# Two packed attentions of a four-layer kernel: their pieces laid anew over the 16 steps of a batch

## The reference

```python
# second layer: attention over moments (instance norm of x comes in at the end)
q = Wq x + bq;  k = Wk kv + bk;  v = Wv kv + bv          # [128 channels, 256]
attn = softmax((q * scale)^T k)                          # per head, 8 channels
mean = attn v;  ex2 = attn (v * v);  std = sqrt(relu(ex2 - mean * mean))
out = (instance_norm(x) * std + mean) * mask

# fourth layer
q = layer_norm((zt + pos)^T);  kv = layer_norm((za + pos)^T)     # per position, over 128 channels
ctx = softmax((q Wq) (kv Wk)^T / sqrt(8)) (kv Wv)
r = ctx Wo + q;  out = (r + gelu(layer_norm(r) W1 + b1) W2 + b2)^T
```

## Time and profile before

| | us | |
|---|---|---|
| median of the runs | 2591.17 | 2588.92 to 2597.12 |
| the profiled execution | 2597.26 | its span 2595.5 |
| TensorE busy | 2261.8 | 87% |
| VectorE busy | 1783.5 | 69% |
| ScalarE busy | 1481.9 | 57% |
| GpSimd busy | 718.5 | 28% |
| exponentials L1405, each | 0.600 | 512 of them |
| maxima L1725, each | 0.684 | 512 of them |

### The profile page before, as it was taken

The page is one execution under the profiler, slowest core; times in us unless marked ns, Lnnn a source line. Parts: engine busy times, 40 slices in busy tenths (PEclk is TensorE's granted clock), DMA queues, the critical chain, the costliest instruction groups (busy, mean ns, idle before and its releaser), DMA issues. The chain is left out here.

```text
span 2595.5 us, 53248 instructions
## 1 busy us (share of the span) xinstructions
PE 2261.8 (87%) x17289; PEld 1802.1 (69%) x17289; DVE 1783.5 (69%) x4693; ACT 1481.9 (57%) x4021; POOL 718.5 (28%) x1041
## 2 busy tenths in 40 slices
PE   4999999995999999979788885899998787888896
PEld 3898989984989899969655553566665784555553
DVE  5666666667666666666577775888886654777746
ACT  2554545553555555557366765677777553666656
POOL 2111111111111111020245442666665104333200
PEclk7999999997999999989799997999999895999978
DMA  4100011000000100010000001000000000000000
GB/s 118 22 21 22 21 22 54 22 21 21 8 23 13 22 21 21 1 33 0 7 10 8 10 5 66 7 0 5 16 15 10 4 5 7 9 8 8 3 3 32
DMA packets 72941, 47.12 MB, mean 18 GB/s; under 512 B 29232, under 2 KB 71601, under 8 KB 72753
## 3 DMA queue, kind: packets, MB, share of 16 engines
q1 hardware_dynamic: 72752, 44.62, 6.5%
HBM read 41.45 MB, written 2.10 MB: 17 GB/s over the span
## 5 line engine op out<-in xcount | busy, mean ns | idle before, releaser
L1725 DVE TENSOR_REDUCE maxima<-bank 128x2 f32<-128x512 f32 x512 | 343.6, 684 | 176.3 <-PE bank L934 174.3
L1405 ACT ACTIVATE probs_t<-bank 128x512 f32<-128x512 f32 x512 | 292.0, 600 | 73.0 <-PE bank L925 68.3
L1281 ACT ACTIVATE wide_probs_t<-bank 128x256 f32<-128x256 f32 x256 | 98.5, 385 | 310.5 <-PE bank L814 308.3
L2047 POOL TENSOR_TENSOR wide_columns<-wide_pair_columns,zero 128x8 f32<-128x8 f32 x16 | 4.4, 278 | 861.4 <-DVE x L1622 816.5
L925 PE MATMUL bank<-q_packed,k_packed 32*128 32x256 f32 x1024 | 209.3, 351 | 31.3 <-ACT probs_t L1405 31.1
L1286 ACT ACTIVATE wide_probs<-bank,wide_neg_max 128x129 f32<-128x129 f32 x512 | 184.1, 365 | 84.7 <-DVE wide_neg_max L1592 80.4
L934 PE MATMUL bank<-k_packed,q_packed 32*128 32x256 f32 x1024 | 209.5, 352 | 8.3 <-DVE k_packed L1738 5.0
L1293 ACT ACTIVATE wide_heads_high<-bank,wide_columns 128x128 fp32r<-128x128 f32 x512 | 160.3, 365 | 96.6 <-PE bank L826 95.3
L925 PEld LDWEIGHTS bank<-q_packed,k_packed 32*128 32x128 f32 x1024 | 127.2, 200 | 120.7 <-ACT probs_t L1405 62.5
L1597 DVE RECIPROCAL wide_inverse<-wide_sums 128x2 f32<-128x2 f32 x256 | 42.5, 166 | 224.6 <-ACT wide_probs L1286 224.6
L1611 DVE SCALAR_TENSOR_TENSOR wide_heads_low<-bank,wide_columns,wide_heads_high 128x128 fp32r<-128x128 f32 x512 | 155.1, 344 | 40.9 <-ACT wide_heads_high L1293 35.5
(11 more groups left out here) (296 smaller groups left out, 6900.5 us busy)
## 6 DMA issues: line engine op xcount, KB each, us to landing
cn<-in_ctx SPq DMA_DIRECT2D x48, 128.0 KB, 2.0
wide_pair_weights<-in_L_xattn_wq SPq DMA_DIRECT2D x16, 256.0 KB, 2.9
wide_pair_weights<-in_L_xattn_wk SPq DMA_DIRECT2D x16, 256.0 KB, 3.3
wide_pair_weights<-in_L_xattn_wv SPq DMA_DIRECT2D x16, 256.0 KB, 3.8
wide_pair_weights<-in_L_xattn_wo SPq DMA_DIRECT2D x16, 256.0 KB, 3.6
q_packed<-max_rows SPq DMA_DIRECT2D x256, 4.0 KB
wide_ctx_rows<-in_ctx SPq DMA_DIRECT2D x4, 512.0 KB, 5.3
x<-in_x SPq DMA_DIRECT2D x4, 512.0 KB, 6.3
```

What stands on the lines that cost most here:

```text
L1405: act.activation(probs_t[j % 8][:, :], shifted_bank[j % 2][:, :], ACT.Exp, bias=0.0).then_inc(s.exp_ready, 1)
L1725: dve.tensor_reduce(maxima[pack // 2][:, b, pack % 2, :], head_scores[packed_scores(1 - u, j)][:, :].rearrange("p (a k) -> p a k", a=UNITS ...
```

## The change

- Each sum of 16 products is cut into two halves of eight, at steps `j % 4 == 2` and `3`; the semaphore is raised after the second. The waits of the sum go to the first half, so that the wait for the copy of the maxima stands at steps 10 and 2.
- Each other piece gets a step of its own as far as there are enough. Second layer: result 0 (now of batch `n-2`), placing q second half 1, k second half 2, projections 4 and 5, turnings 8 and 9, values 12, placing k first half 13, q first half 14. Fourth layer: rows turned 0, placings second half k 1, q 2, projections 4 and 5, turnings 7 and 8, values 9, placings first half k 10, q 11, heads 12, turned back 13, output product 15.
- Fourth layer: adding positions, turning, measuring and norming of rows happen one window earlier (batch `n+5` added, `n+4` turned, measured and normed by roots in window `n`), while turning back stays at batch `n+3`.
- `sums_copy` gets a fifth place, so that the first sum of a batch may be copied before the sums of the batch before are turned.
- GpSimd's order in the second layer is changed: the moments' mask work goes to batch `n-2`, the key work is cut in two around the heads, and the values' work comes last. The key sums on VectorE move from step 12 to 3.

```diff
-SCHEDULE1 = Schedule(place_k=0, project_k=2, turn=(6, 7), values=9, place_q_first=11, place_k_first=14, result=12)
-SCHEDULE3 = Schedule(place_k=1, project_k=3, turn=(6, 7), values=9, place_q_first=11, place_k_first=10, result=15)
+SCHEDULE1 = Schedule(second_q=1, second_k=2, project_q=4, project_k=5, turn=(8, 9), values=12, first_q=14, first_k=13, result=0)
+SCHEDULE3 = Schedule(second_q=2, second_k=1, project_q=4, project_k=5, turn=(7, 8), values=9, first_q=11, first_k=10, result=15)
+PLACED_ROWS, TURNED_BACK, HEADS = 0, 13, 12
+SUMS = (2, 3)
...
+def sums_place(g, u):
+    return PACKS * u if g == 0 else g
...
# TensorE
+                    if third and fourth and j == PLACED_ROWS:
+                        pe.wait_ge(s.placed, 2 * (i + 5))
+                        if following:
+                            pe.wait_ge(s.q_ready, 2 * (n + 1) + 1)
...
+                    if late and not third and j == when.result:
+                        pe.wait_ge(s.heads_ready, UNITS * (n - 1))
...
-                    if j % PACK == LAST_SUMS and (j > LAST_SUMS and core or j == LAST_SUMS and carry):
+                    if j % PACK in SUMS and (j > LAST_SUMS and core or j <= LAST_SUMS and carry):
...
-                        pe.wait_ge(s.exp_ready, HN * n + j - 3)
-                        if j == LAST_SUMS:
-                            pe.wait_ge(s.max_copied, 2 * n + (2 if core else 0))
-                        if j == TURN_MAXIMA[0] + 2 and following:
-                            pe.wait_ge(s.max_copied, 2 * (n + 1) + 1)
-                        if j == HN - 1 and third and carry:
-                            pe.wait_ge(s.heads_copied, i)
-                        for c in range(UNITS):
-                            for m in range(PACK):
+                        c = SUMS.index(j % PACK)
+                        if c == 0:
+                            pe.wait_ge(s.exp_ready, HN * n + PACK * (j // PACK))
+                            if j < LAST_SUMS:
+                                pe.wait_ge(s.max_copied, 2 * n + (2 if core else 0))
+                            if j == TURN_MAXIMA[0] + 1 and following:
+                                pe.wait_ge(s.max_copied, 2 * (n + 1) + 1)
+                            if j > HEADS and third and carry:
+                                pe.wait_ge(s.heads_copied, i)
+                        for m in range(PACK):
+                            last = pe.matmul(sum_bank[quad[m], :], v[:, c, PACK * g + m, :],
+                                             probs_t[(PACK * g + m) % 8][:, c * D:(c + 1) * D], start=c == 0, stop=c == UNITS - 1)
+                        if c:
+                            last.then_inc(s.sums, 1)
+                    if following and j == when.second_q:
+                        pe.wait_ge(s.q_ready, 2 * (n + 1) + 1)
+                        if third and fourth:
+                            pe.wait_ge(s.turned_copied, i + 5)
+                        put("q", 1, upper)
+                    if following and j == when.second_k:
+                        pe.wait_ge(s.k_ready, 2 * (n + 1) + 1)
+                        if late:
+                            pe.wait_ge(s.x_added, n - 1)
...
+                    if ahead and j == when.project_q:
+                        pe.wait_ge(s.in_ready, n + 3)
+                        if following:
+                            pe.wait_ge(s.q_ready, 2 * (n + 1) + 2)
+                        elif third and fourth:
+                            pe.wait_ge(s.turned_copied, i + 5)
...
# ScalarE
-                        if g == 0 and carry:
+                        if g == 1 and carry:
                             act.wait_ge(s.sums_turned, UNITS * n)
...
+                    if third and fourth and j == PLACED_ROWS + 1:
+                        act.wait_ge(s.turned, i + 5)
+                        after(act, s.rows_normed, i + 4)
+                        act.activation(turned_packed[:, :, :].rearrange("p k c -> p (k c)"), upper[:, :], ACT.Copy).then_inc(s.turned_copied, 1)
...
# GpSimd, fourth layer
+                if fifth:
+                    pool.wait_ge(s.loaded[1 - u], pair_turn(1, at(5), 1 - u))
+                    after(pool, s.turned, i + 5)
...
+                if fourth:
-                    pool.wait_ge(s.aggregated, 4 * (i + 4))
+                    pool.wait_ge(s.aggregated, 4 * (i + 5))
...
-                    after(pool, s.turned_back, i + 3)
+                    after(pool, s.turned_back, i + 4)
```

More of the change, by code:

```diff
@@ L954, in window @@
[L954 to L960, removed]
+                        else:
+                            after(pe, s.turned_copied, i + 4)
@@ new lines, in window @@
+                        for m in range(4):
+                            last = pe.transpose(upper[:, m * P:(m + 1) * P], placed_packed[:, m // 2, m % 2 * P:(m % 2 + 1) * P], ident[:, :])
+                        last.then_inc(s.turned, 1)
+                    if late and not third and j == when.result:
+                        pe.wait_ge(s.heads_ready, UNITS * (n - 1))
+                        if following:
+                            pe.wait_ge(s.k_ready, 2 * (n + 1) + 1)
+                        for m in range(2):
+                            for unit in range(UNITS):
+                                last = pe.transpose(lower[:, (2 * m + unit) * P:(2 * m + unit + 1) * P],
+                                                    heads_out[unit][:, m * P:(m + 1) * P], ident[:, :])
+                        last.then_inc(s.result, 1)
@@ L987, in window @@
+                    if ahead and j == when.project_k:
+                        pe.wait_ge(s.in_ready, n + 3)
+                        if following:
+                            pe.wait_ge(s.k_ready, 2 * (n + 1) + 2)
+                        pe.matmul(lower[:, 0:D], w_k, keys_in[u], start=True, stop=True).then_inc(s.k_projected, 1)
                     for unit in range(UNITS):
@@ L1017, in window @@
                         put("q", 0, upper)
[L1018 to L1025, removed]
+                    if ahead and j == when.first_k:
                         pe.wait_ge(s.k_low, n + 3)
                         if carry:
-                            pe.wait_ge(*((s.heads_taken, heads_taken(1, n)) if third else (s.x_added, n)))
+                            pe.wait_ge(s.heads_taken, heads_taken(third, n))
                         put("k", 0, lower)
[L1030 to L1040, removed]
-                        if ahead:
-                            pe.wait_ge(s.q_ready, 2 * (n + 2) + 1)
-                        elif following:
-                            pe.wait_ge(s.v_taken, n + 2)
-                        for k in range(4):
-                            last = pe.transpose(upper[:, k * P:(k + 1) * P], placed_packed[:, k // 2, k % 2 * P:(k % 2 + 1) * P], ident[:, :])
-                        last.then_inc(s.turned, 1)
-                    if third and carry and j == 13:
+                    if third and carry and j == HEADS:
                         pe.wait_ge(s.heads_taken, heads_taken(1, n))
@@ L1054, in window @@
                         last.then_inc(s.heads_turned, 1)
+                    if third and coming and j == TURNED_BACK:
+                        pe.wait_ge(s.rows_normed, i + 4)
+                        if ahead:
+                            pe.wait_ge(s.k_ready, 2 * (n + 2) + 1)
+                        else:
+                            after(pe, s.in_ready, n + 3)
+                        for m in range(4):
+                            last = pe.transpose(lower[:, m * P:(m + 1) * P], norm_packed[:, m // 2, m % 2 * P:(m % 2 + 1) * P], ident[:, :])
+                        last.then_inc(s.turned_back, 1)
                     if third and carry and j == when.result:
@@ L1352, in window @@
                 i = n - B * third
-                core, following, carry, ahead, coming, fourth = (at(o) is not None for o in (0, 1, -1, 2, 3, 4))
+                core, following, carry, ahead, coming, fourth, late = (at(o) is not None for o in (0, 1, -1, 2, 3, 4, -2))
                 for j in range(HN):
```

173 lines of the change are left out of this document (79 added, 94 removed).

## The result

The changed kernel takes 2856.93 us in the median of 4 runs (2818.72 to 2858.20), the kernel before 2592.06 in the median of 4. The ratio is 1.098, 95% interval 1.090 to 1.106: slower by a tenth, far outside the range. The profiled execution is the 2818.72 one; its span is 2817.0 us, 221.5 more than before. It is the quickest of the four: the other three took 2856 to 2858 us at a mean granted clock of 0.817 to 0.821, against 0.836 in the profiled one, so the profile shows the smallest loss of the four.

A forecast was written before the change was run, and what follows sets the result against it. TensorE was taken as fullest but stopping for other engines. First attention -11, second -8, clock -4, beginning +3, ends +0.5 total -20 us: 2577 profiled, 2571 on the median's footing; range 2552 to 2595.

The forecast's parts named there:

- Clock: Falls of TensorE's clock to the lower level, about 1.2 us each; three of four in the second attention go: -4 us.
- the other terms: First attention -11 us, second -8, beginning of the second +3, ends of both attentions +0.5.
- the small term: Second attention: three of its four falls of the clock, about 1.2 us each, taken away, -4 us.
- TensorE's work per batch: TensorE's own work in the new order: 17.9 us per batch in the first attention, 19.3 in the second.
- the wait at step 10: TensorE's first half sum waits for VectorE's copy of the maxima, 0.45 us late in both attentions.
- What remains of the stops: TensorE's stops in the new order: exponentials gone, waits left at step 10 and before the second attention's values, small ones.
- The wait for the norms: Second attention, step 13: the 2.3 us stop of the turning back for GpSimd's norms goes.
- the norms' buffers: Second attention, from step 13: late next, needing 4.5 us against TensorE's 4.6; cost 0.
- the three that I counted: First attention before the change, per batch: 0.9 us for exponentials, 0.7 before values, 0.2 before sums.
- The beginning of the second attention: Before its batch 0, a GpSimd chain is added, less overlap and a 1.5 us wait: +3 us, between -2 and +9.
- Side-by-side steps and the 0.1 us behind each half: First attention: lost overlaps 1.3 us and 0.1 x 4 for divided sums; 1.7 us more on TensorE.
- C: Rival: steps 2 and 10 each wait one maximum of 0.6 us longer, 1.2 per batch; +14, 2605 us; chance 0.14.

The follow-up runs named there:

- Kick0: Changed kernel plus 40 extra unused products in step 0 of batch 0 of each attention: 2574.52 us, ratio 0.989 to the kernel before.
- before_halves: Kernel before with nothing changed but the sums divided in two halves, their waits at the first half: 2728.75 us, ratio 1.050.
- whole_sums: Changed kernel with undivided sums at steps 3, 7, 11, 15, all else as changed: 2533.20 us, ratio 0.975 to the kernel before.

## Why the prediction was wrong, by its own steps

- **The step that failed is "Clock".** I counted the clock as a few falls that stops bring, priced them at 1.2 us each and took three away: -4 us. The true term was a loss of 240 to 280 us: the profiled spans differ by 221.5 us and the medians by 265, and to each come the 16 us that the other terms had promised. Two things should have warned me. The stretch before the second attention stands at 0.51, so each order must first win the higher level; I asked only how often it is lost. And I took the stops of TensorE for the cause of the lower level, though no row showed more than that they went together: the changed order stood at 0.50 with one stop of 0.7 us in 400 us, and the second attention with divided sums in the old order held 1.00 for 220 us with three stops in each batch. Kick0 shows that the clock is the loss; before_halves and whole_sums, the division put in and taken out by itself, show that the divided sums are its main cause (in the old order they cost the level in the first attention only).
- **Within its own bounds the small term was right.** Where the level was held, the four falls of the second attention were gone: in kick0 it stood at 1.00 from 2183 to 2485 us.
- **The rule that I weighed.** The Trainium skill, page "TensorE: Matmul & The Clock Gate", section "HAM oscillation — how this bites in real kernels", says that pauses between groups of products put the clock back each time. The 174 us at 1.00 with almost no stop agree with it; the 220 us at 1.00 with stops of 1.1 us in every batch do not bear it out for pauses of that length. It made me look for the loss in the pauses, and removing them did not keep the level.
- **TensorE's work per batch** was right in its sum, in the second attention by luck. First: 18.5 forecast, 18.7 with the burst, of which the wait at step 10 is 0.6 (0.45 forecast). Second: 20.3 forecast, 20.33 measured. There 1.0 us of the forecast were waits (0.3, 0.45, 0.15 and 0.1), and from start to start kick0 shows about 0.5: 0.3 at step 10, 0.2 before the values, 0.1 before the key placing. TensorE's own work is thus near 19.8 us and not 19.3, about half of the difference in the eight halves of the sums, 0.57 each and not 0.54. The two errors cancel.
- **What remains of the stops** was right in place. The wait for the maxima moved to step 10, 0.5 us in eleven of eleven batches of the first attention; in the second its record is 0.2 us and not 0.45. The wait for the norms is gone, the norms' buffers came in time. In the first attention of the kernel before there were two more stops than the three that I counted, for `std_t` (0.3 us in nine batches) and `k_packed` (0.2 us in seven).
- **The beginning of the second attention**, +3 forecast: from the first placed rows to batch 0 it took 53.7 us before and 53.4 after, so nothing.
- **What I gave away without weighing it**: that the division itself is a loss. Side-by-side steps and the 0.1 us behind each half stood in the sum as 1.7 us, and I set them against the stops as one parcel with the rest of the change. Taken apart, the division alone cost 1.0 and 1.1 us per batch at full clock, and the spreading of the pieces with whole sums gains 1.6 and 1.8. The stop at step 10 was no reason to divide either: whole sums have one of up to 0.8 us at step 11, and their batches are still the shorter.
- **The rivals.** C had the sign but not the mechanism: neither step 2 nor step 10 waited longer than thought. No rival had an order that is never granted the clock.

What stays open: why the level came back in the second attention at 2559 us after six batches of the same steps at the lower one, why it never did in the first, and why one run in four with the burst lost it. That where a stretch falls in time decides is a guess; no experiment here shows it. Nor do the runs say why whole sums bring the level and halves do not. Theory S, the unbroken length of the work on all rows, fits all of them in the main, but no run changes the length alone with the amount of that work and the length of a batch kept.

## What to carry to other kernels

Look first at which clock level a stage is entered, and ask of a new order of TensorE's work whether it has stretches like those that brought the level up in the old one; an order that is good at full clock can stay at half, and its profile then shows a TensorE that is 99% busy and hardly waits. Be slow to divide a long run of full-row products to even out steps: here the evenness of the rest could be had without it, and the division was a loss even at full clock. When a change has several parts, price each alone.

## What the runs showed of the hardware

- With TensorE busy for 472.8 of 476 us the granted clock was 0.50 throughout, in products of 32 and 128 rows that alternate every 0.7 to 1.1 us.
- Forty products of 128 x 128 by 256 in a row, 6.6 us, brought the higher level; four in each of 16 steps over 46 us did not.
- At the higher level the same order held it for 174 us, and with a burst ahead for 303 us, without one fall. Stops of 0.8 to 1.1 us in every batch did not bring a fall in 220 us of the old order with divided sums.
- Adding 80 products to the changed kernel made it 282 us faster in the median, adding 1024 made it 121 us faster.
- The same 16 products of each sum, in one run of 1.00 us or in two of 0.57 us a step apart, made the difference between a granted clock of 0.95 and of 0.50 in the first attention.
